# Last two stages of a conditioned residual stack fused over batch rows, with the residual kept time-innermost

## The chip, the cores and the metric

The kernel runs on one core of one Trainium2 chip. The metric is the device time of one execution, in microseconds (us); before the change it is the median of 3 runs. The profile is one further execution, taken by the hardware profiler. Engines are named as in the profile: PE (TensorE's matmuls), PEld (TensorE's weight loads), DVE (VectorE), ACT (ScalarE), POOL (GpSimd), SP (SyncE, which issues most DMAs).

## The reference

The input x is (16, 512, 512): batch B, time T, channels D, all float32; `cond` is (16, 512). Four layers are applied, each added to x:

```
x = x + ssm(x)      # causal conv (4 taps), softplus/tanh gates of 64 states, linear scan over time, projection to D
x = x + lstm(x)     # a = x Wx + h Wh + b; i,f,o = sigmoid, g = tanh; c = f c + i g; h = o tanh(c); h0 = cond
x = x + moe(x)      # below
x = x + masked(x)   # below

def moe(x):         # E=16 experts, slot = e_idx*C + position, C = 512, rows past capacity are dropped
    xprev = concat([cond[:, None], x[:, :-1]], axis=1)
    xk, xr = x + (xprev - x) * maa_k, x + (xprev - x) * maa_r
    rows = zeros(E*C + 1, D).at[slot].set(xk)
    out  = square(relu(rows @ w_key)) @ w_value          # per expert
    return sigmoid(xr @ w_recept.T) * out[slot]

def masked(x):      # over time, for each batch row and channel
    ax = abs(x);  pi = exp(2 * ax / sum(ax));  cum = cumsum(pi / sum(pi)) + 0.001
    chosen = sum(cum <= rv)                              # rv = cond
    return x * (ax >= ax[chosen])
```

The residual after the LSTM is called x2 below, after the experts x3. The last layer needs, for each batch row and channel, all 512 times of x3.

## The kernel before, in words

Four stages run one after the other, with a barrier over all engines at the end of each. Channels lie on the 128 partitions in KD = 4 blocks. Within an engine instructions run in the order in which they are written in its list; engines hand over by semaphores. Loops over tiles are hardware loops (`Fori`) with the first and last tiles unrolled. Large fp32 products of tiles are made from three fp32r products of a high and a low part (`split_products`, L837 to L842).

**`recur_phase`** (L105 to L834) walks through time in 32 tiles of 16 steps; a tile has 256 tokens, time-major (t, b). Each LSTM step, in two halves of the hidden channels, is a chain: PE's recurrent products (`recur`, L425), VectorE's transposes out of PSUM (`turn`, L696) and sum with the input products (`add_inputs`, L701), ScalarE's tanh (L586, L587), VectorE's cell (`new_cell`, L707 to L713), ScalarE's tanh of it (L589), VectorE's hidden state (`new_hidden`, L718), and back to PE. All else is put beside it as filler, by tables that say in which step of a tile each piece is issued: `CONV_AT` (convolution products L625/L629 for the tile three ahead, on VectorE), `SCAN_AT` (five parts of the state scan, L635 to L667), `BLOCK_AT` (`add_block` L683, first residual sum into the `stream` tile), `SPLIT_AT` (high part L523 on ACT; POOL makes the low part, `split_low` L293), `KEEP_X2_AT` (`keep_x2` L691: x2 into the stream tile, one instruction of 512 elements for each half tile), `PROJECT_AT`, `INPUTS_AT`, `OUTPUTS_AT` (PE's products, L375 to L396), ACT's copy of the input products (`keep_inputs` L528, every step), and, for the tile before, `SCALE_AT`, `TURN_AT`, `ROWS_AT`: the token shift for the experts. That shift is, for each half tile: POOL subtracts (`mix_shift` L303), ACT scales (`scale_shift` L534), POOL adds (`mix_add` L308), PE transposes to token rows (`turn_rows` L406), ACT copies them out (`keep_rows` L542), POOL scatters them to the expert rows in DRAM by the slot table (`scatter`, L315 and L321). There are four `stream` tiles in a ring, (KD, 16 + 256): the 16 leading columns, the halo, are the last time of the tile before, copied by POOL (L341). SP stores each tile's x2 to DRAM in its token order (L238) and loads the windows of later tiles.

**`expert_phase`** (L845 to L1035) multiplies the 16 experts. It is not changed.

**`combine_phase`** (L1038 to L1251, "gating stage") walks over 32 tiles of 256 tokens: ACT and VectorE mix the token with the one before, split it in high and low parts, PE makes the receptance in three products of four blocks, each in its own PSUM bank, ACT the sigmoid (L1194), POOL gathers expert rows by the slot table, PE transposes them, VectorE multiplies and adds into x3, which stays in SBUF, (KD, B, T) with time innermost (`times`; written at a stride, L1246).

**`mask_phase`** (L1254 to L1425, "last stage") walks over 64 units, one batch row and channel block each, of 512 times: ACT takes |x| and its sum (L1335), VectorE halves and inverts the sum (L1378, L1384), ACT makes the exponent into PSUM with its sum (L1343), VectorE the running sum (`scan` L1388) and the threshold (`bound` L1394), ACT counts times below the threshold by the sum of signs (L1351), VectorE turns that into an index (L1408), picks the value at it (`search` L1413) and makes the factor 1 or 2 (L1420), POOL multiplies (L1326), SP stores (L1306).

## Time and profile before

| | us |
|---|---|
| median of 3 runs (range) | 4221.14 (4220.53 to 4221.26) |
| the profiled execution | 4221.9 |
| its span | 4220.2 |
| PE busy in the span | 3814.3 (90%) |
| DVE busy | 3103.0 (74%) |
| ACT busy | 1798.7 (43%) |
| POOL busy | 590.7 (14%) |

The span runs from the first to the last recorded instruction. The shares are means over stages with different limits, so rows are given by stretch below. The recurrence runs from 122 to 3013 us, the experts up to 3808, the gating stage from there to 4036.6, the last stage to the end. Busy PE is not PE at its peak; "granted clock" (PEclk) is the share of its full clock that TensorE was given.

### The profile page before, as it was taken

To read this page: it belongs to the slowest core of one execution; us is meant where nothing else is said; L and a number is where in the kernel's file an instruction comes from. 1 tells how busy PE (TensorE), PEld (TensorE's weight loads), DVE (VectorE), ACT (ScalarE), POOL (GpSimd) and SP (SyncE) were. 2 spreads that over 40 slices of the span, in tenths; PEclk is the share of its full clock that TensorE was granted. 3 is DMA by queue.
4 is the path that set the end of the run, shared out by engine and by line. 5 is a ranking of instruction groups with operands and counts; after the bars stand their busy time and mean duration, and the time that the engine had idled before them with its cause. 6 is when DMAs were issued, how large, how long until landed. Compare 5 with 4: busy or idle time off the path is not lost. (4 is left out here: it accounts for less than half of the span.)

```text
span 4220.2 us, 116142 instructions
## 1 busy us (share of the span) xinstructions
PE 3814.3 (90%) x45058; PEld 2616.4 (62%) x45058; DVE 3103.0 (74%) x9922; ACT 1798.7 (43%) x5526; POOL 590.7 (14%) x653
## 2 busy tenths in 40 slices
PE   3999999999999999999999999999599999997920
PEld 3566666666656666665666666665378887887920
DVE  9877888787878787887878788855455445537989
ACT  3334333334333334433333433333244344437877
POOL 2011101111101110110111110110100000004644
PEclk9999999999999999999999999999899999998965
DMA  7110010110010110010001001000233433324422
GB/s 276 31 36 27 29 31 27 34 36 27 29 32 27 32 39 27 26 34 27 29 31 36 27 29 31 25 21 12 94 131 122 161 135 119 122 84 156 164 83 97
DMA packets 143096, 267.78 MB, mean 63 GB/s; under 512 B 19606, under 2 KB 85654, under 8 KB 139540
## 3 DMA queue, kind: packets, MB, share of 16 engines
q1 hardware_dynamic: 120896, 185.19, 13.1%
q0 software_dynamic: 17696, 66.79, 4.3%
q10 hardware_dynamic: 4020, 9.10, 0.6%
q8 instruction: 335, 5.49, 0.6%
q14 instruction: 149, 1.22, 0.1%
HBM read 177.46 MB, written 83.92 MB: 62 GB/s over the span
## 5 line engine op out<-in xcount | busy, mean ns | idle before, releaser
L425 PE MATMUL bank<-buf,buf 128*16 128x256 f32 x32768 | 1871.9, 380 | 78.5 <-DVE buf L718 65.4
L425 PEld LDWEIGHTS bank<-buf,buf 128*16 128x16 f32 x32768 | 905.9, 97 | 903.3 <-DVE buf L718 116.0
L840 PE MATMUL bank<-buf,buf 128*128 128x256 f32 (+1 forms) x3584 | 1183.1, 330 | 29.8 <-DVE buf L1225 22.4
L841 PE MATMUL bank<-buf,buf 128*128 128x256 f32 (+1 forms) x3584 | 1122.7, 313 | 0.0
L842 PE MATMUL bank<-buf,buf 128*128 128x256 f32 (+1 forms) x3584 | 1122.3, 313 | 0.0
L629 DVE SCALAR_TENSOR_TENSOR buf<-buf,buf,buf 128x256 f32<-128x256 f32 x1920 | 871.9, 481 | 1.6 <-issue 1.6
L840 PEld LDWEIGHTS bank<-buf,buf 128*128 128x128 f32 x3584 | 678.9, 189 | 279.9 <-issue 241.8
L696 DVE STREAM_TRANSPOSE buf<-bank 128x256 f32<-128x256 f32 x1024 | 459.0, 448 | 510.3 <-PE bank L425 479.7
L586 ACT ACTIVATE buf<-buf 128x96 f32<-128x96 f32 x1024 | 290.5, 284 | 1161.5 <-DVE buf L701 1160.9
L842 PEld LDWEIGHTS bank<-buf,buf 128*128 128x128 f32 x3584 | 680.5, 190 | 41.2
L841 PEld LDWEIGHTS bank<-buf,buf 128*128 128x128 f32 x3584 | 681.7, 190 | 38.5
L589 ACT ACTIVATE buf<-buf 128x32 f32<-128x32 f32 x1024 | 235.0, 229 | 628.2 <-DVE buf L713 628.2
L701 DVE SCALAR_TENSOR_TENSOR buf<-buf,buf 128x128 f32<-128x128 f32 x1024 | 368.6, 360 | 20.0
L1023 DVE CAST buf<-buf 128x512 fp32r<-128x512 f32 x128 | 54.7, 427 | 355.6 <-ACT buf L983 352.5
L308 POOL TENSOR_TENSOR buf<-buf,buf 128x512 f32<-128x512 f32 x64 | 81.8, 1279 | 1477.1 <-ACT buf L534 1477.1
L528 ACT ACTIVATE buf<-bank,buf 128x256 f32<-128x256 f32 x512 | 234.7, 458 | 21.9 <-PE bank L842 20.9
L718 DVE SCALAR_TENSOR_TENSOR buf<-buf,buf 128x32 f32<-128x32 f32 x1024 | 194.2, 190 | 61.4 <-ACT buf L589 14.2
L713 DVE SCALAR_TENSOR_TENSOR buf<-buf,buf 128x32 f32<-128x32 f32 x1024 | 196.6, 192 | 36.6 <-DVE buf L710 1.4
L587 ACT ACTIVATE buf<-buf 128x32 f32<-128x32 f32 x1024 | 217.9, 213 | 0.0
L707 DVE SCALAR_TENSOR_TENSOR buf<-buf,buf 128x32 f32<-128x32 f32 x1024 | 179.5, 175 | 18.2 <-ACT buf L586 15.1
L710 DVE SCALAR_TENSOR_TENSOR buf<-buf,buf 128x32 f32<-128x32 f32 x1024 | 190.0, 186 | 0.0
L293 POOL TENSOR_TENSOR buf<-buf,buf 128x512 fp32r<-128x512 f32 x64 | 82.1, 1284 | 559.3 <-ACT buf L523 559.3
(143 smaller groups left out, 3040.3 us busy)
## 6 DMA issues: line engine op xcount, KB each, us to landing
buf<-in_wk SPq DMA_DIRECT2D x16, 2048.0 KB, 9.6
buf<-in_wv SPq DMA_DIRECT2D x16, 2048.0 KB, 9.7
buf<-in_xT SPq DMA_DIRECT2D x62, 496.0 KB, 3.8
buf<-x_scratch SPq DMA_DIRECT2D x31, 544.0 KB, 4.2
buf<-in_xT SPq DMA_DIRECT2D x32, 512.0 KB, 3.7
expert_in_scratch<-buf POOLq DMA_DIRECT2D x16, 1024.0 KB, 22.2
x_scratch<-buf SPq DMA_DIRECT2D x32, 512.0 KB, 5.0
buf<-expert_in_scratch SPq DMA_DIRECT2D x16, 1024.0 KB, 11.6
```

Of the source, the lines that this page charges most:

```text
L425: last = mm(gate_ps[hf][32 * j:32 * j + B, 0:HCOLS], hist[:, k, at_step(slot_at)], wh[:, k, j * GCOLS + hf * HCOLS:j * GCOLS + (hf + 1) * ...
L528: a(xw[par][:, :, q, :], xw_ps[q % 2][:, 0:LTILE].rearrange("p (t b) -> p t b", b=B), ACT.Identity, bias=bias[:, q:q + 1]).then_inc(s["xw_ ...
L586: a(gate[hf], pre[hf][:, 0:6, :], ACT.Tanh, scale=0.5).then_inc(s["ifo_ready"][hf], 1)
L587: a(gcand[hf], pre[hf][:, 6:8, :], ACT.Tanh).then_inc(s["g_ready"][hf], 1)
L589: a(tanh_c[hf], cell[hf], ACT.Tanh, scale=0.5).then_inc(s["tc_ready"][hf], 1)
L629: v.scalar_tensor_tensor(out=conv[:, k, :], in0=src, scalar=taps[:, k, i:i + 1], in1=conv[:, k, :], op0=ALU.mult, op1=ALU.add).then_inc(s[ ...
L696: v.transpose(turned_g[hf].rearrange("p g b -> p (g b)"), gate_ps[hf][:, 0:HCOLS])\
L701: v.scalar_tensor_tensor(out=pre[hf], in0=turned_g[hf][:, :, 0:B], scalar=0.5, in1=xw[par][:, st, 8 * hf:8 * hf + 8, :], op0=ALU.mult, op1 ...
L713: v.scalar_tensor_tensor(out=cell[hf], in0=term_f[hf], scalar=0.5, in1=term_i[hf], op0=ALU.mult, op1=ALU.add).then_inc(s["c_ready"][hf], 1)
L840: nc.tensor.matmul(out, left[0], right[0], start=first, stop=False)
L841: nc.tensor.matmul(out, left[0], right[1], start=False, stop=False)
L842: return nc.tensor.matmul(out, left[1], right[0], start=False, stop=last)
```

## The change

`x2` in DRAM becomes (partition, channel block, batch row, time), and the `stream` tiles (KD, B, 1 + 16): time innermost, rows of 17 words with the halo as the first. All that writes or reads them follows: tokens of a tile are now ordered (b, t) for the input, state and mixing products, while the recurrence's own history and convolution stay time-major, so some operands are read at a stride. SP's store of a tile's x2 becomes 8192 runs of 64 bytes. The token shift is made by ACT (`weigh_last`: last times maa_k) and VectorE (`mix_in`: now times 1 - maa_k, plus that), four instructions each for a half tile; the low parts of the split go from POOL to VectorE; `keep_x2` is four instructions a half. POOL keeps the halo copies and scatters. The slot table is reloaded in (b, t) order, and a second one, `place`, in batch-row order.

`combine_phase` and `mask_phase` go; `finish_phase` takes their place, fully unrolled over the 16 batch rows, with a ring of six row buffers. Its receptance is plain fp32 products of 512 columns (in four passes of PE) into two banks, without splits; the sigmoid is a tanh of half the value, with the halving in VectorE's product. ACT's Tanh and Exp, VectorE's scans and POOL's products of neighbouring rows are interleaved in written-out orders.

```diff
-    x2_d = nc.dram_tensor("x2_scratch", (KD, P, NTOK), F32, kind="Internal").ap()
+    x2_d = nc.dram_tensor("x2_scratch", (P, KD, B, T), F32, kind="Internal").ap()
...
-    stream = [carve(KD, B + LTILE) for _ in range(4)]
+    stream = [carve(KD, B, 1 + LSTEPS) for _ in range(4)]
...
-    CONV_AT = [[0, 5, 10, 15, 18, 21, 24, 28, 32], [0, 4, 9, 14, 18, 21, 24, 29, 32]]
+    CONV_AT = [[0, 5, 10, 15, 18, 21, 24, 28, 32], [0, 5, 10, 13, 17, 20, 23, 27, 32]]
...
-    SCALE_AT, TURN_AT, ROWS_AT = (4, 10), (5, 13), (6, 14)
+    SCALE_AT, MIX_AT, TURN_AT, ROWS_AT = (4, 9), (5, 10), (6, 13), (7, 14)
+    LOW_AT = (13, 14)
...
+            sp.dma_start(place, slot_d.rearrange("(c p) -> p c", p=P), allow_slow_non_contiguous=True)\
...
-                    sp.dma_start(x2_d.rearrange("c p n -> p c n")[:, :, bass.ds((n - 1) * LTILE, LTILE)],
-                                 stream[four - 1][:, :, B:]).then_inc(s["x2_stored"][(four + 1) % 2], 16)
+                    sp.dma_start(x2_d.rearrange("p c b t -> p (c b) t")[:, :, bass.ds((n - 1) * LSTEPS, LSTEPS)],
+                                 stream[four - 1].rearrange("p c b t -> p (c b) t")[:, :, 1:])\
...
-                g.tensor_tensor(mix, stream[four][:, :, u * P:u * P + P], stream[four][:, :, B + u * P:B + u * P + P],
-                                ALU.subtract).then_inc(s["shift_ready"], 1)
...
             def keep_inputs(m, par, q):
-                a(xw[par][:, :, q, :], xw_ps[q % 2][:, 0:LTILE].rearrange("p (t b) -> p t b", b=B), ACT.Identity,
+                a(xw[par][:, :, q, :], xw_ps[q % 2][:, 0:LTILE].rearrange("p (b t) -> p t b", b=B), ACT.Identity,
...
+            def weigh_last(m, four, u):
+                for k in range(KD):
+                    a(mix[:, k, :].rearrange("p (b t) -> p b t", b=B), stream[four][:, k, :, 8 * u:8 * u + 8],
+                      ACT.Copy, scale=maa_k[:, k:k + 1])\
...
             def keep_x2(n, four, u):
-                v.scalar_tensor_tensor(out=kept, in0=hist[:, :, tok], scalar=0.5, in1=kept, op0=ALU.mult,
-                                       op1=ALU.add).then_inc(s["x2_done"], 1)
+                for k in range(KD):
+                    kept = stream[four][:, k, :, 8 * u + 1:8 * u + 9]
+                    last = v.scalar_tensor_tensor(
+                        out=kept, in0=hist[:, k, u * P:(u + 1) * P].rearrange("p (t b) -> p b t", b=B), scalar=0.5,
+                        in1=kept, op0=ALU.mult, op1=ALU.add)
...
+            def mix_in(m, four, u):
+                for k in range(KD):
+                    part = mix[:, k, :].rearrange("p (b t) -> p b t", b=B)
+                    v.scalar_tensor_tensor(out=part, in0=stream[four][:, k, :, 8 * u + 1:8 * u + 9],
+                                           scalar=maa_now[:, k:k + 1], in1=part, op0=ALU.mult,
+                                           op1=ALU.add).then_inc(s["mixed"], 1)
...
+def finish_phase(nc, ctx, ins, carve, banks, keep, x2_d, y_d, out):
+    RING, NC = 6, T // P
+    r_ps, t_ps, pi = banks[0:2], banks[2:6], banks[6:8]
...
+            def receptance(i):                                             # PE
+                pe.wait_ge(s["xr_ready"], KD * (i + 1))
+                for m in range(KD):
+                    if i >= 1 or m >= 2:
+                        pe.wait_ge(s["gate_ready"], KD * i + m - 1)
+                    for k in range(KD):
+                        last = nc.tensor.matmul(r_ps[m % 2][:, 0:T], wr[:, k, m * P:(m + 1) * P], xr[i % 2][:, k, :],
+                                                start=k == 0, stop=k == KD - 1)
+                    last.then_inc(s["r_summed"], 1)
...
+            receptance(0)
+            turn(0)
+            receptance(1)
+            turn(1)
+            receptance(2)
+            for i in range(B):
+                if i + 2 < B:
+                    turn(i + 2)
+                if i + 3 < B:
+                    receptance(i + 3)
...
+            def open_gate(i):                                              # ACT
+                for m in range(KD):
+                    act.wait_ge(s["r_summed"], KD * i + m + 1)
+                    a(gate[i % 2][:, m, :], r_ps[m % 2][:, 0:T], ACT.Tanh, scale=0.5).then_inc(s["gate_ready"], 1)
...
+            def exponent(i):                                               # ACT
+                act.wait_ge(s["inv_ready"], i + 1)
+                for k in range(KD):
+                    if i >= 1 or k >= 2:
+                        act.wait_ge(s["cum_ready"], KD * i + k - 1)
+                    a(pi[k % 2][:, 0:T], ax[i % 2][:, k, 0:T], ACT.Exp, scale=column(inv, i, k),
+                      accum_out=column(pi_sum, i, k)).then_inc(s["pi_ready"], 1)
...
+            for i in range(B):                                             # ACT
+                take_sides(i)
+                if i + 1 < B:
+                    absolute(i + 1)
+                if i + 2 < B:
+                    open_gate(i + 2)
+                if i + 1 < B:
+                    exponent(i + 1)
+                if i + 4 < B:
+                    weigh_last(i + 4)
...
+            def combine(i):                                                # DVE
+                for k in range(KD):
+                    u = KD * i + k
+                    dve.wait_ge(s["gate_ready"], u + 1)
+                    dve.wait_ge(s["turned"], u + 1)
+                    v.scalar_tensor_tensor(out=gated[k % 2], in0=gate[i % 2][:, k, :], scalar=1.0, in1=t_ps[k][:, 0:T],
+                                           op0=ALU.add, op1=ALU.mult).then_inc(s["gated_ready"], 1)
+                    dve.wait_ge(s["gated_ready"], u + 1)
+                    v.scalar_tensor_tensor(out=x2_of(i, k), in0=gated[k % 2], scalar=0.5, in1=x2_of(i, k),
+                                           op0=ALU.mult, op1=ALU.add).then_inc(s["x3_ready"], 1)
...
+            for i in range(B):                                             # DVE
+                scan(i)
+                bound(i)
+                if i + 1 < B:
+                    combine(i + 1)
+                if i + 3 < B:
+                    mix_in(i + 3)
+                choose(i)
+                if i + 1 < B:
+                    invert(i + 1)
+                search(i)
+                keep(i)
```

`scan`, `bound`, `choose`, `search` and `keep` do for the four blocks of a row what the old stage did for a unit. POOL gathers the expert rows of row i + 3, then makes the four products of row i; SP loads a row's x2 as soon as its ring buffer is free and stores each finished block.

## Rows read from the trace of the kernel before

**Rows 1.** Windows by stage: stretch, us, busy us of PE, PEld, DVE, ACT, POOL, PEclk, DMA share, GB/s.
```profile
122.00:3013.00 2891.00, 2815.33 (x39600) 1760.76 (x39600) 2239.94 (x8305) 1108.62 (x4210) 316.28 (x340) 1.00 0.09 29
3808.30:4036.60 228.30, 210.80 (x1792) 210.38 (x1792) 202.71 (x293) 185.78 (x357) 126.30 (x129) 0.96 0.48 156
4036.60:4220.20 183.60, 0.00 (x0) 0.00 (x0) 170.97 (x513) 143.99 (x385) 82.35 (x70) 0.50 0.24 91
```
**Rows 2.** Timeline in one recurrence tile: start, us, instruction, count, [idle before, releaser].
```profile
1336.47 0.65 DVE L640 SCALAR_TENSOR_TENSOR buf<-bank,buf,buf 64x256 f32<-64x256 f32 x1
...
1337.85 0.45 DVE L696 STREAM_TRANSPOSE buf<-bank 128x256 f32<-128x256 f32 x1 [0.72 <-PE bank L425]
...
1343.04 0.45 DVE L696 STREAM_TRANSPOSE buf<-bank 128x256 f32<-128x256 f32 x1
1343.53 1.84 DVE L701 SCALAR_TENSOR_TENSOR buf<-buf,buf 128x128 f32<-128x128 f32 x1
1343.90 1.30 POOL L303 TENSOR_TENSOR buf<-buf 128x512 f32<-128x512 f32 x1
...
1349.94 0.44 DVE L696 STREAM_TRANSPOSE buf<-bank 128x256 f32<-128x256 f32 x1
...
1383.28 0.45 DVE L696 STREAM_TRANSPOSE buf<-bank 128x256 f32<-128x256 f32 x1 [1.71 <-PE bank L425]
...
1389.68 0.45 DVE L696 STREAM_TRANSPOSE buf<-bank 128x256 f32<-128x256 f32 x1 [1.67 <-PE bank L425]
...
1393.09 0.48 DVE L629 SCALAR_TENSOR_TENSOR buf<-buf,buf,buf 128x256 f32<-128x256 f32 x1
1393.48 0.68 DVE L691 SCALAR_TENSOR_TENSOR buf<-buf,buf 128x512 f32<-128x512 f32 x1
...
1394.73 0.45 DVE L696 STREAM_TRANSPOSE buf<-bank 128x256 f32<-128x256 f32 x1 [0.57 <-PE bank L425]
1395.29 0.79 DVE L701 SCALAR_TENSOR_TENSOR buf<-buf,buf 128x128 f32<-128x128 f32 x1
```
**Rows 3.** VectorE's groups, 150 to 2740 us: count | busy us, mean ns | idle before.
```profile
L629 DVE SCALAR_TENSOR_TENSOR buf<-buf,buf,buf 128x256 f32<-128x256 f32 x1711 | 785.9, 481 | 1.6 <-issue 1.6
L691 DVE SCALAR_TENSOR_TENSOR buf<-buf,buf 128x512 f32<-128x512 f32 x57 | 38.7, 679 | 0.0
L640 DVE SCALAR_TENSOR_TENSOR buf<-bank,buf,buf 64x256 f32<-64x256 f32 x29 | 18.8, 648 | 0.0
L635 DVE TENSOR_TENSOR buf<-buf,buf 64x256 f32<-64x256 f32 x29 | 11.9, 410 | 0.0
```
**Rows 4.** Timeline: the gating stage's first work, the last scan.
```profile
3814.32 2.19 ACT L1162 ACTIVATE buf<-buf 128x512 fp32r<-128x512 f32 x4 [14.29 <-DMA buf<-in_maa_r]
...
4211.31 1.21 DVE L1388 TENSOR_TENSOR_SCAN buf<-buf,bank 128x512 f32<-128x512 f32 x1
```
**Rows 5.** Groups by line and shape over the whole span, last stage.
```profile
L1413 DVE SCALAR_TENSOR_TENSOR buf<-buf,buf,buf 128x513 f32<-128x513 f32 x64 | 48.8, 762 | 0.0
L1343 ACT ACTIVATE bank<-buf,buf 128x512 f32<-128x512 f32 x64 | 44.2, 691 | 27.2 <-DVE buf L1384 27.2
L1420 DVE TENSOR_SCALAR buf<-buf,buf 128x512 f32<-128x512 f32 x64 | 31.1, 487 | 0.9
```
**Rows 6.** PE's timeline in one recurrence tile.
```profile
1312.25 1.03 PE L375 MATMUL bank<-buf,buf 128*128 128x256 f32 x4
```
**Rows 7.** Windows around two pauses of PE, columns as in rows 1.
```profile
58.10:61.90 3.80, 0.01 (x1) 0.01 (x1) 3.80 (x5) 1.23 (x2) 2.69 (x3) 0.80 0.36 116
61.90:67.20 5.30, 5.28 (x25) 5.30 (x26) 5.30 (x15) 0.47 (x1) 5.30 (x10) 0.50 0.84 325
...
3821.80:3825.20 3.40, 3.37 (x16) 3.40 (x17) 1.67 (x4) 2.79 (x6) 0.00 (x0) 0.50 0.40 94
```
**Rows 8.** The page's DMA issues: count, KB each, median us from issue to landing.
```profile
buf<-in_wk SPq DMA_DIRECT2D x16, 2048.0 KB, 9.6
```
**Rows 9.** The page's DMA queues: packets, MB, share of 16 engines' span.
```profile
q1 hardware_dynamic: 120896, 185.19, 13.1%
```

More of the change, by code:

```diff
@@ L522, in split_high @@
                     act.wait_ge(s["xw_summed"], NBLK * (m - 1))
[L523 removed]
+                a(x1_hi[four % 2][:, two(q), :].rearrange("p k (b t) -> p (k b) t", b=B),
+                  stream[four][:, two(q), :, 1:].rearrange("p k b t -> p (k b) t"), ACT.Copy)\
                     .then_inc(s["x1_hi_ready"], 1)
@@ L796, in _ @@
             for q in range(2):
+                split_low(0, 0, q)
+            for q in range(2):
                 convolve(1, q, 0, CONVS // 2)
@@ L802, in _ @@
                 add_block(1, 0, 1, q)
+            for q in range(2):
+                split_low(1, 1, q)
             convolve(2, 1, 0, CONVS // 2)
@@ L830, in tile @@
                         add_block(n + 2, pair + 1, (four + 2) % 4, BLOCK_AT.index(st))
+                    if ahead >= 2 and st in LOW_AT:
+                        split_low(n + 2, (four + 2) % 4, LOW_AT.index(st))
+                    if later(n, 1) and st in MIX_AT:
+                        mix_in(n - 1, (four - 1) % 4, MIX_AT.index(st))
                     if st in KEEP_X2_AT:
@@ L834, in _ @@
             tiles(dve, tile)
+            for u in range(2):
+                mix_in(NLT - 1, 3, u)
 def split_products(nc, out, left, right, first, last):
@@ L1156, in _, with turn @@
-            tiles(pe, tile)
+            def turn(i):
+                for c in range(NC):
+                    pe.wait_ge(gathered[NC * (i % 2) + c], 16 * (i // 2 + 1))
+                for k in range(KD):
+                    if i >= 1:
+                        pe.wait_ge(s["gated_ready"], KD * (i - 1) + k + 1)
+                    for c in range(NC):
+                        last = nc.tensor.transpose(t_ps[k][:, c * P:(c + 1) * P],
+                                                   rows[i % 2][c][:, k * P:(k + 1) * P], ident)
+                    last.then_inc(s["turned"], 1)
@@ L1199, in _, with weigh_last @@
-            tiles(act, tile)
+            a = nc.scalar.activation
+            def weigh_last(i):
+                act.wait_ge(landed[i % RING], 16 * (i // RING + 1))
+                act.wait_ge(s["halo_ready"], i + 1)
+                for k in range(KD):
+                    if i >= 1:
+                        act.wait_ge(s["xr_ready"], KD * (i - 1) + k + 1)
+                    a(weighed[:, k, :], stream[i % RING][:, k, 0:T], ACT.Copy, scale=maa_r[:, k:k + 1])\
+                        .then_inc(s["weighed"], 1)
@@ new lines, in _ @@
+            act.wait_ge(s["weights_landed"], 32)
+            weigh_last(0)
+            weigh_last(1)
+            open_gate(0)
+            weigh_last(2)
+            absolute(0)
+            open_gate(1)
+            exponent(0)
+            weigh_last(3)
+            for i in range(B):
+                take_sides(i)
[7 more added lines that the diff above has]
+                    weigh_last(i + 4)
@@ new lines, in bound, with choose, search @@
+            def bound(i):
+                dve.wait_ge(s["cum_ready"], KD * (i + 1))
+                v.tensor_tensor(limit[i % 2], rv[:, :, i], pi_sum[i % 2], ALU.mult).then_inc(s["limit_ready"], 1)
+            def choose(i):
+                dve.wait_ge(s["sides_ready"], KD * (i + 1))
+                v.tensor_scalar(chosen[i % 2], sides[i % 2], 0.5, T / 2, ALU.mult, ALU.add)\
+                    .then_inc(s["chosen_ready"], 1)
+            def search(i):
+                dve.wait_ge(s["chosen_ready"], i + 1)
+                for k in range(KD):
+                    v.scalar_tensor_tensor(out=flag[:, k, :], in0=places, scalar=column(chosen, i, k), in1=ax[i % 2][:, k, :],
+                                           op0=ALU.is_equal, op1=ALU.mult, accum_out=column(level, i, k))\
+                        .then_inc(s["level_ready"], 1)
```

539 lines of the change are left out of this document (176 added, 363 removed).

## The prediction

> **What bounds the kernel now.** I read the busy times by stage first, then the vector engine's timeline inside one tile of the recurrence, then the last two stages. The page's 90% for PE hides three limits. The recurrence takes 2891 of 4220.2 us; PE runs at full clock, but each of its 512 steps is a chain PE, VectorE, ScalarE, VectorE, PE, and VectorE has about 22% idle [rows 1]. The gating stage takes 228.3 us, 210.8 of them PE; the last stage takes 183.6 us without PE, VectorE busy for 171.0 [rows 1]. So a bound by PE is followed by one by VectorE, and overlapping them is what can be won. The expert stage between is untouched.
>
> **The recurrence, part by part.** A plain step lasts 5.19 us, from one first transpose L696 to the next (1337.85 to 1343.04) [rows 2]; I number steps 0 to 15 in a tile. Step 7 lasts 6.90 (from 1343.04), since L701 takes 1.84 (at VectorE's rate, below, it is worth 0.28) while POOL's subtraction L303 runs for 1.30, and the fill behind it then ends late [rows 2]. Step 14 carries the same kind of extra PE products without that block and lasts 6.40 (1383.28 to 1389.68); step 15 lasts 5.05 [rows 2].
> Removed: six POOL products of this kind a tile. Step 7 falls to step 14's 6.40, so -0.5; the blocked L701 of step 0 (0.79 instead of 0.28) gives back some 0.4 [rows 2].
> Moved: PE's row transposes from step 5 to 6, which I take as neutral. Step 5 would then last 5.19, but VectorE gets four mixing products (128 elements, pointer scalar). L629 takes 0.481 for 256; L691 and L635 differ by 0.269 for 256 elements, 1.05 ns each, so 128 elements take 0.347 [rows 3]. Neighbours overlap by some 0.08 (L629 of 1393.09 takes 0.48, and L691 behind it starts after 0.39 [rows 2]), so four take 1.14. They stand behind L640 (1336.47, minus the 0.45 by which step 5's own block shifts it), so step 5 ends 0.3 later than 5.19.
> Step 15: two more convolution products, 0.4 each, move L691's place from 1393.48 to 1394.28 [rows 2], and its second half becomes four instructions of 128. L691 takes 0.679 for 512 [rows 3], so 0.28 for 128, 0.20 apart. One operand is now read at a stride of 64 bytes; L640, which writes at that stride, takes 0.648 for 256 where L635 takes 0.410, of which 0.06 is the pointer scalar [rows 3]: some 0.6 ns an element, so 0.08 each. The four start 0.28 apart and the last takes 0.36, so they end at 1395.48; the next transpose, at 1394.73 before, overlaps them by 0.08 and starts 0.67 late.
> Steps 10 to 14 also get work (four products, the residual sums at up to 1.0, two splits of 0.68), within the 0.5 to 1.7 us that VectorE waits for PE there: at 1389.68 it had waited 1.67 [rows 2]. Without that cover they would cost 3 us a tile.
>
> Sum a tile: -0.5 - 0.4 + 0.3 + 0.67 = +0.07, times 28 tiles +2 us. Bounds: stride for nothing gives -8; every stream operand (rows of 17 words) at the stride's price +20. I take +2. ScalarE's copies of input products read PSUM at a 64-byte stride; only those ahead of the table loads in step 3 lie on the path: 0 to 0.15 x 28; I take all of it, +4. The start has four more VectorE splits and fewer POOL blocks: -3 to +4, taken as 0. At the end the last scatter no longer waits for two pairs of POOL products, 1.3 each, replaced by VectorE's 1.1, partly overlapped: -3. SP also issues each tile's residual store, now 8192 runs of 64 bytes, and a second slot table; window loads queued behind have some 40 us to spare, and the last store lies beside the scatters (priced among the rivals). Recurrence: +3 us.
>
> **The fused stage.** One batch row (512 tokens) replaces two gating tiles and four mask units. VectorE per row: four mixing products 0.66 apart (2.7), four dependent pairs at 0.60 each and 0.11 for the operand in PSUM, an estimate (5.3, from L691 [rows 3]), four scans 1.13 apart (4.6, L1388 [rows 4]), four searches 0.70 apart (2.8, L1413 [rows 5]), four factors (1.6, L1420 [rows 5]), small ones 0.8: 17.8 us. PE: an fp32 product is four passes; two of 256 columns are the four records of L375 in 1.03, 0.43 each to issue [rows 6], so 0.86 for 512; sixteen make 13.8, transposes about 2: 15.8 at full clock. ScalarE: twenty instructions at 0.6 to 0.7 (L1343 [rows 5]): 13.
>
> None of these sets the period; the order does. ScalarE's order is sides of row i, absolute of i+1, gate of i+2, exponent of i+1. Receptance has two banks, so PE stops after two blocks of row i+2 until ScalarE has opened gate 0, and gates 2 and 3 then wait for PE, one after the other, with the exponent queued behind them and VectorE's scan behind that. The cycle: scan 4.6, limit 0.25, combine 5.3, last absolute 0.7, gate 0 0.6, two PE blocks 6.9, gate 3 0.6, first exponent 0.75, six hand-overs 0.4 (estimate) = 20.1 us. VectorE's mixing, search and factors (7.5) run beside PE's blocks. The added wait is this one, and PE itself idles 20.1 - 15.8 = 4.3 us a row.
>
> That idle time costs clock. After 3.80 us without a product PE is at 0.50 for the next 5.3 us; at the gating stage's first products it is at 0.50 for 3.4 us [rows 7]. Half speed over 3.4 us puts 1.7 us on the two blocks, which lie on the cycle: 21.8 us a row (22.7 with the 5.3).
>
> Start: the weights were there at 3814.3 [rows 4]; one more MB loads ahead of them, half of the 9.6 us that 2 MB take [rows 8]: 3819.1. Mixing 3.4, receptance of row 0 13.8 + 1.7 at half clock, transposes 2, receptance of row 1 13.8, gate 0.8, exponent 0.75: first scan at 3855.4. Row 15's scan follows 14 periods and one short iteration (no gate left: 15.9) later. From the last scan to the end the old kernel needs 4220.2 - 4211.3 = 8.9 [rows 4]; with four units in each step 3 x (1.13 + 0.72 + 0.70 + 1.27) more: 20.4. End: 3855.4 + 14 x 21.8 + 15.9 + 20.4 = 4196.9, so 411.9 has become 388.6.
>
> **Sum.** 4196.9 + 3 = 4199.9. The profiled execution took 4221.9, 1.7 beyond its span and 0.8 above the median of 4221.14, so I forecast 4202 us, 0.45% less.
>
> **Rivals.**
> First, the clock holds, as gaps below 4.3 us may go unpunished: 20.1 a row, 4197 - 24 + 5 = 4178. Against it stands the drop after 3.80 us [rows 7]. Bound 4165.
> Second, the small stores cost like other packets. The page's main queue spends 13.1% of 16 engines' span on 120896 packets, 73 ns each [rows 9]; 8192 / 16 such packets take 37 us. Within a tile of 90 us that hides, but the last store then lands near 3055 and the stage, which ended at 3035 (new: 3032), waits: +23, so 4225. No row shows writes of 64 bytes. The Trainium skill (DMA: Bandwidth & Descriptors, Specifications) speaks against this layout too: below 512 bytes a transfer does a read-modify-write, so each 64-byte run would cost a read beside its write. By that rule the last store is at least late in this way, and no row of this trace shows it.
> Third, slower: PE's clock does not come back within the two blocks. Place: blocks 2 and 3 of each row's receptance. If PE stays at half for both, they take 13.8 instead of 6.9, the period is 27.0, and the time 3891.7 + 14 x 27.0 + 4.7 = 4274. It decides from 23.3 us a row, where PE is at half for 6.3 us after each gap; the rows have 3.4 and 5.3 [rows 7], which speaks against it, but never with a gap in every row.
> Fourth, the strided operands cost their upper bound: +18, 4220, no change.
>
> POOL's final products (1.3 each) may hold up VectorE's factors as L303 holds up L701 [rows 2]: at most 3.8 on 17.8, still below 21.8, so it would show only beside rival 1, as 21.6 a row.
>
> **Chances.** Forecast 47% (its own range 4190 to 4215, the upper end at 22.7 a row), rival 1 18%, rival 2 10%, rival 3 13%, rival 4 7%, something else 5%. No change means within 0.2%, 8.4 us, about what a measurement of this kernel can tell: 4212.7 to 4229.6. Faster: 44 + 18 + 1 = 63%; same: 3 + 9 + 6 = 18%; slower: 13 + 1 + 1 + 4 = 19%. For 8 in 10 the range goes from inside rival 1 to past rivals 2 and 4: 4168 to 4234.
>
> **What would show it.** After: scans of successive rows 21 to 22 us apart; PE idle some 4 us in each, ended by ScalarE's gate, and the granted clock below 1.0 there; ScalarE waiting for PE in two of four gates; VectorE idle before each row's first scan; L701 never above 0.4 except beside POOL's short copies; step 15 near 5.7, step 7 near 6.4; the expert stage beginning within 5 us of 3035. Rows 20 us apart at full clock mean rival 1; a gap of 20 us before the expert stage, ended by the residual's store, rival 2; rows 24 us or more apart rival 3. I am wrong in kind if VectorE has no idle time in the fused stage, or if the recurrence moves by more than 20 us.

## The result, and the profile after

The changed kernel takes 4194.43 us (median of 4 runs, 4192.25 to 4197.63) where the kernel before takes 4221.2 (4220.53 to 4221.46): a ratio of 0.9937, 95% interval 0.992 to 0.9955, 27 us less. The forecast was 4202 with a range of its own of 4190 to 4215, so the time lies inside. The stages show that two terms missed it in opposite directions, by 17 and by 11 us. The table compares the two traced executions; the one traced after the change is the slowest of its four, 3.2 us above their median, so its spans differ by 25.3 us and not by 27.

| us, from the two traces | before | after | forecast of the difference |
|---|---|---|---|
| first step's first transpose | 121.98 | 120.34 | 0 |
| last step's first transpose | 3008.68 | 2997.42 | +6 |
| expert stage's first load | 3035.49 | 3021.67 | +3, measured -13.8 |
| first DMA behind the experts | 3808.37 | 3795.01 | +3 |
| from there to the end | 411.8 | 399.9 | -23.3, measured -11.9 |
| span | 4220.2 | 4194.9 | -20, measured -25.3 |

The expert stage between is as long as before (772.9 and 773.3). First two windows of the kernel after: the recurrence, and the rows of the fused stage from the first row's first scan to the last row's (stretch, us, busy us of PE, PEld, DVE, ACT, POOL, PEclk, DMA share, GB/s). They answer to [rows 1].

```profile
120.34:3002.60 2882.26, 2815.95 (x39600) 1761.56 (x39600) 2316.79 (x8808) 1111.99 (x4212) 83.91 (x156) 1.00 0.14 29
3844.90:4156.00 311.10, 252.14 (x675) 119.79 (x674) 261.14 (x445) 178.67 (x445) 123.73 (x118) 0.88 0.37 125
```

In the recurrence VectorE has 77 us more to do and POOL 232 us less, in a slightly shorter stretch. In the 311 us of rows no engine is full: VectorE, which is busy for 84%, comes nearest, and PE's granted clock is 0.88.

VectorE's timeline in the same tile as [rows 2], transposes that begin steps 5, 6, 7, 8, 14, 15 and the next step 0, and the residual sums in step 15:

```profile
1327.21 0.45 DVE L682 STREAM_TRANSPOSE buf<-bank 128x256 f32<-128x256 f32 x1 [0.84 <-PE bank L387]
1332.60 0.43 DVE L682 STREAM_TRANSPOSE buf<-bank 128x256 f32<-128x256 f32 x1
1338.04 0.45 DVE L682 STREAM_TRANSPOSE buf<-bank 128x256 f32<-128x256 f32 x1 [0.30 <-PE bank L387]
1344.47 0.45 DVE L682 STREAM_TRANSPOSE buf<-bank 128x256 f32<-128x256 f32 x1 [0.41 <-PE bank L387]
...
1377.82 0.45 DVE L682 STREAM_TRANSPOSE buf<-bank 128x256 f32<-128x256 f32 x1 [1.10 <-PE bank L387]
1384.23 0.45 DVE L682 STREAM_TRANSPOSE buf<-bank 128x256 f32<-128x256 f32 x1 [1.46 <-PE bank L387]
...
1388.82 1.20 DVE L659 SCALAR_TENSOR_TENSOR buf<-buf,buf 128x128 f32<-128x128 f32 x4
1389.94 0.44 DVE L682 STREAM_TRANSPOSE buf<-bank 128x256 f32<-128x256 f32 x1
```

Steps 5, 6, 7, 14 and 15 last 5.39, 5.44, 6.43, 6.41 and 5.71. By medians over the tiles (before, then after): step 0 5.53 and 5.15, step 5 5.64 and 5.38, step 6 5.19 and 5.45, step 7 6.91 and 6.44, step 15 5.06 and 5.72; all others within 0.03. A tile goes from 90.30 to 90.12.

VectorE's groups in the recurrence, 150 to 2740 us (count | busy us, mean ns | idle before): the sum of the chain that was held up (L701 before, L687 now), the residual sums and the mixing products.

```profile
L701 DVE SCALAR_TENSOR_TENSOR buf<-buf,buf 128x128 f32<-128x128 f32 x912 | 330.7, 363 | 17.7
...
L687 DVE SCALAR_TENSOR_TENSOR buf<-buf,buf 128x128 f32<-128x128 f32 x916 | 264.7, 289 | 18.9 <-DVE buf L682 1.4
L659 DVE SCALAR_TENSOR_TENSOR buf<-buf,buf 128x128 f32<-128x128 f32 x228 | 68.2, 357 | 0.0
L676 DVE SCALAR_TENSOR_TENSOR buf<-buf,buf,buf 128x128 f32<-128x128 f32 x224 | 62.8, 339 | 0.0
```

Before the change 82 of the 912 sums took over 0.15 us longer than their median of 0.29, 67 us in all; after it none does. The held sums stand in step 0 (0.40 longer), step 7 (1.55) and, which the prediction's sum leaves out, step 5: there POOL's second product of the shift held a sum in each of 28 tiles, by 0.45. From the same tile before:

```profile
1332.01 1.28 POOL L308 TENSOR_TENSOR buf<-buf,buf 128x512 f32<-128x512 f32 x1 [26.46 <-ACT buf L534]
...
1332.69 0.75 DVE L701 SCALAR_TENSOR_TENSOR buf<-buf,buf 128x128 f32<-128x128 f32 x1
```

Now the fused stage. VectorE's first scans of three rows, and PE's and ScalarE's timeline between them:

```profile
3978.51 4.55 DVE L1274 TENSOR_TENSOR_SCAN buf<-buf,bank 128x512 f32<-128x512 f32 x4 [3.70 <-ACT bank L1203]
...
4000.12 4.55 DVE L1274 TENSOR_TENSOR_SCAN buf<-buf,bank 128x512 f32<-128x512 f32 x4 [2.57 <-ACT bank L1203]
...
4022.87 1.22 DVE L1274 TENSOR_TENSOR_SCAN buf<-buf,bank 128x512 f32<-128x512 f32 x1 [3.72 <-ACT bank L1203]
```
```profile
3976.98 1.91 PE L1154 MATMUL bank<-buf,buf 128*128 128x128 f32 x16
3978.72 7.03 PE L1143 MATMUL bank<-buf,buf 128*128 128x512 f32 x16
3989.94 8.81 PE L1143 MATMUL bank<-buf,buf 128*128 128x512 f32 x16 [4.19 <-ACT buf L1188]
3998.59 1.91 PE L1154 MATMUL bank<-buf,buf 128*128 128x128 f32 x16
4000.34 7.03 PE L1143 MATMUL bank<-buf,buf 128*128 128x512 f32 x16
4011.56 9.94 PE L1143 MATMUL bank<-buf,buf 128*128 128x512 f32 x16 [4.19 <-ACT buf L1188]
```
```profile
3989.32 1.05 ACT L1188 ACTIVATE buf<-bank 128x512 f32<-128x512 f32 x2
3995.36 0.60 ACT L1188 ACTIVATE buf<-bank 128x512 f32<-128x512 f32 x1 [4.99 <-PE bank L1143]
3998.79 0.60 ACT L1188 ACTIVATE buf<-bank 128x512 f32<-128x512 f32 x1 [2.84 <-PE bank L1143]
3999.28 0.69 ACT L1203 ACTIVATE bank<-buf,buf 128x512 f32<-128x512 f32 x1
```

This is the cycle of the prediction, step for step: PE makes two blocks, stops for 4.19 us until ScalarE opens gate 0 (the tanh of the receptance's first block); two more blocks follow, gates 2 and 3 wait for them (4.99 and 2.84), the exponent stands behind gate 3 and VectorE's scan, idle for 2.6 or 3.7, behind the exponent. Rows come 21.61 and 22.75 us apart, in turn. The same two blocks take 7.03 in one place and 8.81 or 9.94 behind the pause. The windows of two pauses and of what follows them:

```profile
3985.80:3989.90 4.10, 0.00 (x0) 0.00 (x0) 4.03 (x8) 4.10 (x14) 0.00 (x0) 1.00 0.13 46
3989.90:3993.40 3.50, 3.46 (x4) 1.51 (x5) 3.46 (x11) 0.47 (x1) 0.00 (x0) 0.51 0.00 0
...
4007.40:4011.50 4.10, 0.00 (x0) 0.00 (x0) 4.03 (x8) 4.10 (x14) 0.00 (x0) 0.87 0.12 50
4011.50:4018.20 6.70, 6.64 (x9) 2.90 (x10) 6.67 (x18) 0.58 (x3) 1.83 (x2) 0.57 0.00 0
```

The granted clock is at the lower level (1.2 of 2.4 GHz) for 3.5 us behind one pause and for most of 6.7 behind the next. Where it held at the upper level (an experiment below) gate 3 came 7.80 us behind gate 0; here 9.46 or 10.60, so the clock costs 1.66 or 2.80 a row.

### The profile page after: what moved, and what is told of

Same layout as the page of the kernel before. It is cut to its first block and busy times, and to the rows that moved or that the text cites. A ratio compares the mean times of both kernels' runs of the same rounds, so it can differ in the third digit from the quotient of the medians.

```text
span 4194.9 us, 112126 instructions
## 1 busy us (share of the span) xinstructions
PE 3890.3 (93%) x44034; PEld 2542.4 (61%) x44034; DVE 3109.5 (74%) x10143; ACT 1679.4 (40%) x5296; POOL 289.2 (7%) x410
## 3 DMA queue, kind: packets, MB, share of 16 engines
q1 hardware_dynamic: 366416, 184.21, 16.4%
## 5 line engine op out<-in xcount | busy, mean ns | idle before, releaser
L837 PE MATMUL bank<-buf,buf 128*128 128x256 f32 (+1 forms) x3072 | 1037.1, 338 | 4.0 <-DVE buf L1008 2.7
L838 PE MATMUL bank<-buf,buf 128*128 128x256 f32 (+1 forms) x3072 | 979.0, 319 | 0.0
L839 PE MATMUL bank<-buf,buf 128*128 128x256 f32 (+1 forms) x3072 | 978.4, 318 | 0.0
L837 PEld LDWEIGHTS bank<-buf,buf 128*128 128x128 f32 x3072 | 582.0, 189 | 254.6 <-issue 216.3
L839 PEld LDWEIGHTS bank<-buf,buf 128*128 128x128 f32 x3072 | 583.9, 190 | 41.2
L838 PEld LDWEIGHTS bank<-buf,buf 128*128 128x128 f32 x3072 | 584.7, 190 | 38.5
L1143 PE MATMUL bank<-buf,buf 128*128 128x512 f32 x512 | 259.6, 666 | 85.2 <-ACT buf L1188 59.0
L687 DVE SCALAR_TENSOR_TENSOR buf<-buf,buf 128x128 f32<-128x128 f32 x1024 | 295.9, 289 | 21.0 <-DVE buf L682 1.4
L1143 PEld LDWEIGHTS bank<-buf,buf 128*128 128x128 f32 x512 | 107.5, 216 | 226.0 <-issue 155.5
L704 DVE SCALAR_TENSOR_TENSOR buf<-buf,buf 128x32 f32<-128x32 f32 x1024 | 193.7, 189 | 61.7 <-ACT buf L557 14.2
L298 POOL DMA_INDIRECT expert_in_scratch<-buf,buf x64 | 63.4, 991 | 2415.3 <-ACT buf L510 2372.5
L699 DVE SCALAR_TENSOR_TENSOR buf<-buf,buf 128x32 f32<-128x32 f32 x1024 | 196.7, 192 | 35.9 <-DVE buf L696 0.6
L693 DVE SCALAR_TENSOR_TENSOR buf<-buf,buf 128x32 f32<-128x32 f32 x1024 | 177.5, 173 | 17.9 <-ACT buf L554 14.8
## 6 DMA issues: line engine op xcount, KB each, us to landing
expert_in_scratch<-buf POOLq DMA_DIRECT2D x16, 1024.0 KB, 22.7
```

What stands on the lines that cost most here:

```text
L687: v.scalar_tensor_tensor(out=pre[hf], in0=turned_g[hf][:, :, 0:B], scalar=0.5, in1=xw[par][:, st, 8 * hf:8 * hf + 8, :], op0=ALU.mult, op1 ...
L837: nc.tensor.matmul(out, left[0], right[0], start=first, stop=False)
L838: nc.tensor.matmul(out, left[0], right[1], start=False, stop=False)
L839: return nc.tensor.matmul(out, left[1], right[0], start=False, stop=last)
L1143: last = nc.tensor.matmul(r_ps[m % 2][:, 0:T], wr[:, k, m * P:(m + 1) * P], xr[i % 2][:, k, :], start=k == 0, stop=k == KD - 1)
```

## The experiments

Each ratio is to the kernel before on the same chip, whose own median lay between 4220.2 and 4223.8 from group to group of runs; the changed kernel's own ratio is 0.9937. Times of different groups are compared with the changed kernel's 4194.4, so differences of 2 or 3 us between groups are not read.

### Which part gave what

The changed recurrence with the old last stages:

```diff
-        finish_phase(nc, ctx, ins, carve, banks, keep, x2_d, y_d, out)
+        combine_phase(nc, ctx, ins, carve, banks, keep, x2_d, y_d)
+        mask_phase(nc, ctx, carve, banks, keep, out)
...
-    x2v = x2_d.rearrange("c p n -> p c n")
+    x2v = x2_d.rearrange("p c b t -> p c (b t)")
```

> The changed recurrence with the gating stage and the last stage of before behind it; the gating stage reads the residual's new layout as if it were the old one, so the values are not the reference's, the work is. Theory (the two parts add, read from the stage bounds of the two traces: expert stage starts at 3021.7 instead of 3035.5, last two stages 399.9 instead of 411.9): the expert stage starts within 1.5 us of 3021.7, the last two stages take 412 again, the time is 4221.2 - 13.8 = 4207 us (4204 to 4211). Rival (the recurrence as the prediction had it, +3): 4224. Rival (all of the gain is in the fused stage, the earlier expert start is of this one profile): 4221.

4208.03 us, ratio 0.9965 (0.9952 to 0.9977), 15 us less than before. The expert stage starts at 3018.1, 3.6 us ahead of the expected 3021.7 where 1.5 was allowed, and the last two stages take 412.8 again. So somewhat over half of the gain is the recurrence's, for which the prediction had +3.

### What holds the rows of the fused stage

First the clock. PE's transposes are moved into the pause, so that the pause becomes short:

```diff
                 for m in range(KD):
+                    if m == 2:
+                        turn(i)
                     if i >= 1 or m >= 2:
```

> The changed kernel with PE's transposes of a row moved from behind its receptance to between its blocks 1 and 2, into the pause of 4.19 us. Theory (the pause costs clock: blocks 2 and 3 take 1.9 or 3.0 us more than at full clock): the pause shrinks to about 1.5 us, the granted clock stays at 1.00, blocks 2 and 3 take 6.9 to 7.0 us, rows come 19.7 us apart instead of 21.6 and 22.75, and the time is 4194.4 - 14 x 2.45 = 4160 us (4156 to 4166). Rival (the transposes stand on the cycle themselves, no clock): rows 20.4 apart with blocks as long as before, 4170. Rival (neither counts, PE has 2.6 us of room elsewhere): 22.2 us a row, 4194.

4196.12 us, 0.9937 (0.992 to 0.9953): no change. The theory in this form fell. PE's timeline and windows around gate 0:

```profile
3981.56 0.63 PE L1156 MATMUL bank<-buf,buf 128*128 128x128 f32 x4
3982.79 0.66 PE L1156 MATMUL bank<-buf,buf 128*128 128x128 f32 x4 [0.61 <-DVE buf L1249]
3984.12 0.66 PE L1156 MATMUL bank<-buf,buf 128*128 128x128 f32 x4 [0.67 <-DVE buf L1249]
3985.44 0.66 PE L1156 MATMUL bank<-buf,buf 128*128 128x128 f32 x4 [0.67 <-DVE buf L1249]
3987.45 15.70 PE L1145 MATMUL bank<-buf,buf 128*128 128x512 f32 x32 [1.36 <-ACT buf L1182]
```
```profile
3981.50:3987.45 5.95, 2.62 (x17) 1.68 (x16) 5.85 (x10) 5.95 (x19) 0.00 (x0) 1.00 0.13 44
3987.45:3994.40 6.95, 6.95 (x12) 2.96 (x13) 6.92 (x17) 1.02 (x2) 2.12 (x2) 0.75 0.00 0
4003.10:4009.09 5.99, 2.65 (x17) 1.68 (x16) 5.89 (x10) 5.99 (x19) 0.01 (x1) 0.93 0.36 128
4009.09:4016.00 6.91, 6.91 (x10) 2.91 (x11) 6.88 (x17) 0.66 (x2) 2.09 (x2) 0.57 0.00 0
```

No pause is longer than 1.36 us, and yet the clock falls to 0.75 and 0.57 over the next 6.9 us: ahead of gate 0 PE worked for 2.6 of 5.9 us. Two of its rows came 19.93 us apart, the others 21.6 to 23.0. That left it open whether the clock is the cause at all. So the pause was filled instead, with products whose results nobody reads:

```diff
                     if m == 2:
+                        if i >= 1:
+                            pe.wait_ge(s["gated_ready"], KD * (i - 1) + 1)
+                            nc.tensor.matmul(t_ps[0][:, 0:T], wr[:, 0, 0:P], xr[i % 2][:, 0, 0:T], start=True, stop=True)
...
                         turn(i)
```

> The kernel with the transposes in the pause, and ahead of them PE products whose results nobody reads (two of 512 columns and one of 256, into a transpose bank that is free by then), so that PE has no pause left before gate 0. Theory (what the rows lose is clock; with the transposes alone the clock still fell in most rows, because PE was busy in only 2.6 of the 5.9 us ahead of gate 0, and the one row group where it held came 19.9 us apart): the granted clock stays at 1.00 from row to row, blocks 2 and 3 take 6.9 us, rows come 19.7 us apart, time 4194.4 - 14 x 2.5 = 4160 us (4156 to 4166), though PE does 2.1 us more work a row. Rival (the length of blocks 2 and 3 has another cause, such as the order of waits around gate 0): 21.6 to 23.0 a row as before, 4195. Rival (more work on PE delays gate 2): above 4195.

4166.86 us, 0.9874 (0.9858 to 0.9891), 28 us below the changed kernel, though PE does more. The window over the whole of its rows, and one pause that is filled:

```profile
3812.30:4126.30 314.00, 288.32 (x855) 139.60 (x853) 271.92 (x462) 189.94 (x469) 127.72 (x122) 1.00 0.39 136
```
```profile
3990.60:3996.70 6.10, 4.49 (x24) 2.88 (x23) 5.96 (x11) 6.10 (x19) 1.47 (x2) 1.00 0.66 246
3996.70:4003.60 6.90, 6.90 (x16) 3.12 (x17) 6.87 (x17) 0.99 (x2) 2.11 (x2) 1.00 0.00 0
```

The clock stays at 1.00 throughout, and rows come 19.94 us apart, 13 of 14 within 0.07. Against the run before it only PE products and a wait ahead of them were added, so the clock is shown to be what the rows lost. That is the cycle at full clock. The expected 19.7 had taken the cost of the clock from PE's merged durations (1.9 and 3.0); from gate 0 to gate 3 it is 1.66 and 2.80, and 21.61 and 22.75 less these are 19.95.

Then ScalarE's order, which makes the cycle:

```diff
-                if i + 2 < B:
-                    open_gate(i + 2)
-                if i + 1 < B:
-                    exponent(i + 1)
+                for blocks in ((0, 1), (2, 3)):
+                    if i + 2 < B:
+                        open_gate(i + 2, blocks)
+                    if i + 1 < B:
+                        exponent(i + 1, blocks)
```

> The changed kernel with ScalarE's order gates 0 and 1, exponents 0 and 1, gates 2 and 3, exponents 2 and 3, instead of four gates and four exponents. Theory (the cycle runs through gates 2 and 3 that stand ahead of the exponents): the first scan of a row no longer waits for them; VectorE, 19.0 us busy a row with its waits for POOL's products, becomes the limit, or exponent 2 behind gate 3 at 19.7 to 20.8 where the clock still falls. Rows 19.0 to 20.3 us apart, time 4194.4 - 14 x (2.0 to 3.2) = 4150 to 4167 us, middle 4158. Rival (PE's slow clock sets the rows, whatever ScalarE's order): 22.2 us a row, 4194.

4156.17 us, 0.9843 (0.9826 to 0.9859): 38 us below the changed kernel, by two exponents a row put ahead of two gates. Rows come 19.1 apart on the mean. The window shows the new bound: VectorE is busy for 195.4 of 200 us, with the clock still at 0.94: rows are 18.95 apart where it holds and up to 19.4 where it falls.

```profile
3900.00:4100.00 200.00, 175.20 (x504) 84.50 (x503) 195.44 (x331) 134.02 (x332) 94.94 (x90) 0.94 0.43 152
```

Both of these edits together:

> The changed kernel with both orders (transposes in the pause, exponents 0 and 1 ahead of gates 2 and 3), POOL's products where the change has them. Theory (VectorE sets the rows, 19.0 us with the factors waiting for POOL's products): rows 19.0 us apart, factors 0.90 us on the mean, time 4194.4 - 14 x 3.15 = 4150 us (4146 to 4156). Rival (the products cost nothing in any order, as in the changed kernel, where VectorE has 2.6 to 3.7 us idle a row): 17.5 a row, 4130.

4158.84 us, 0.9848 (0.982 to 0.9877): no better than the early exponents alone. Rows at 18.95 are there, but between them some of 20.8 to 21.0, where the clock fell, so the mean is 19.2. The expected 19.0 had left the clock out.

With VectorE as the bound, POOL's products count, which hold up the factors (0.897 us on the mean in the changed kernel's rows, 0.487 before [rows 5]):

```profile
L1298 DVE TENSOR_SCALAR buf<-buf,buf 128x512 f32<-128x512 f32 x56 | 46.8, 897 | 0.0
```

```diff
-                    pool.wait_ge(s["factor_ready"], KD * i + k + 1)
+                    pool.wait_ge(s["factor_ready"], KD * i + (KD if i + 1 < B else k + 1))
```

> Both of these orders together, and POOL's four products of a row held back until VectorE has made all four factors, so that they run beside its scans (in the trace of before 62 scans ran beside such products at 1.205 us, as long as without). Theory (then VectorE alone sets the rows; a factor takes 0.49 instead of 0.90 us without the products beside it): rows 17.4 to 17.8 us apart, VectorE without idle time, time 4194.4 - 14 x 4.6 = 4130 us (4124 to 4138). Rival (the products block VectorE wherever they stand, then its products of gate and rows): 19.0 a row, 4150. Rival (PE or the clock still sets the rows): 19.7 or more, above 4158.

> The kernel with exponents 0 and 1 ahead of gates 2 and 3 and late products, the transposes where the change has them. Theory (moving the transposes gained nothing in the changed kernel and lost 2.7 us beside the early exponents; late products take 1.6 us a row from VectorE): 4156.2 - 14 x (1.0 to 1.6) = 4134 to 4143 us. Rival (the clock falls in every row and sets the rows by gate 3 and exponent 2): 19.0 a row, 4154.

4142.73 (0.9809, 0.9793 to 0.9826) with both orders, 4141.11 (0.9813, 0.9797 to 0.9829) with the transposes left in place. The late products are worth 16 us behind both orders and 13 to 15 behind the early exponents alone, the move of the transposes again nothing. Rows are 17.66 apart where the clock holds and 19.4 where it falls; with both orders the time is above the expected 4124 to 4138, which had taken the clock to hold. At last all of these edits together, with two unread PE products of 512 columns a row in the pause:

> The kernel with both orders and late products, and two PE products of 512 columns that nobody reads ahead of the transposes in the pause. Theory (its rows were 17.66 apart where the clock held and 19.4 where it fell, mean 18.2): all rows 17.7 apart, VectorE busy in 17.3 of them, time 4142.7 - 14 x 0.55 = 4135 us (4131 to 4140). Rival (PE, now busy for 17.3 us a row, becomes late itself): 18.2 or more, 4143 or above.

4136.32 us, 0.98 (0.9784 to 0.9816), the fastest of all, 58 us below the changed kernel. Windows, and VectorE's factors and scans and POOL's products in the same stretch:

```profile
3900.00:4100.00 200.00, 195.14 (x580) 95.25 (x578) 191.47 (x357) 142.01 (x354) 96.39 (x96) 1.00 0.44 157
```
```profile
L1273 DVE TENSOR_TENSOR_SCAN buf<-buf,bank 128x512 f32<-128x512 f32 x47 | 54.8, 1206 | 5.2 <-ACT bank L1201 5.2
L1297 DVE TENSOR_SCALAR buf<-buf,buf 128x512 f32<-128x512 f32 x48 | 20.0, 480 | 0.0
...
L1129 POOL TENSOR_TENSOR buf<-buf,buf 128x512 f32<-128x512 f32 x48 | 55.2, 1182 | 92.5 <-DVE buf L1297 92.5
```

The factors are back at 0.48, and the scans, beside which the products now run, take 1.206, no longer than the 1.20 of the changed kernel. PE and VectorE are both at 96 to 98%, and VectorE is idle for under 0.8 us a row, so another order has little left to win.

### What moved in the recurrence

The row transposes of the first half, in steps 8 and 9 instead of 6 and 7 (`TURN_AT`, `ROWS_AT`):

```diff
-    SCALE_AT, MIX_AT, TURN_AT, ROWS_AT = (4, 9), (5, 10), (6, 13), (7, 14)
+    SCALE_AT, MIX_AT, TURN_AT, ROWS_AT = (4, 9), (5, 10), (8, 13), (9, 14)
```

> The changed kernel with the first half's row transposes in step 8 and their copy in step 9, instead of 6 and 7. Theory (the transposes cost the step that holds them 0.25 us of the chain, which the prediction took as nothing): step 6 falls from 5.45 to 5.20, step 8 rises from 5.07 to some 5.3, step 7 stays at 6.44, the time unchanged within 3 us. Rival (step 6 is longer for another reason, VectorE's mixing products in step 5): step 6 stays at 5.45. Rival (step 7's extra length is ScalarE's row copy): step 7 falls below 6.3.

4194.5 us, 0.9928 (0.9906 to 0.9951), no change in time. Step 6 falls from 5.45 to 5.06, step 7 from 6.44 to 6.19, step 8 rises from 5.07 to 5.65. The transposes do cost the step that holds them; that step 7 falls as well may be due to the copy, as the last rival has it, or to what step 6 had left over, which this run does not tell apart.

The strided operand, taken away in one place (the history is read contiguously):

```diff
-                        out=kept, in0=hist[:, k, u * P:(u + 1) * P].rearrange("p (t b) -> p b t", b=B), scalar=0.5,
+                        out=kept, in0=hist[:, k, u * P:(u + 1) * P].rearrange("p (b t) -> p b t", b=B), scalar=0.5,
```

> The changed kernel with the history operand of the residual sums read contiguously instead of at a stride of 64 bytes (other tokens' values, so the output is not the reference's; same count of instructions and elements). Theory (the stride costs VectorE some 0.08 us for 128 elements, and step 15 waits for it): the sums take 0.28 instead of 0.357 us, step 15 lasts 5.72 - 0.32 = 5.40, 28 tiles make -9 us: 4185. Rival (their length is from the pointer or the short rows of the other operand): 0.357 and 5.72 stay, 4194.

4185.6 us, 0.9912 (0.9883 to 0.994). The residual sums take 0.282 instead of 0.357, step 15 5.41 instead of 5.72, a tile 0.33 less: theory and number hold. The group in the recurrence:

```profile
L659 DVE SCALAR_TENSOR_TENSOR buf<-buf,buf 128x128 f32<-128x128 f32 x232 | 51.5, 282 | 0.0
```

POOL's work was put back in two pieces. The low-part subtraction (`split_low`), again on POOL:

```diff
-                    if ahead >= 2 and st in LOW_AT:
-                        split_low(n + 2, (four + 2) % 4, LOW_AT.index(st))
...
+                g.tensor_tensor(x1_lo[four % 2][:, two(q), :].rearrange("p k (b t) -> p (k b) t", b=B),
...
+                if ahead >= 2:
+                    for q in range(2):
+                        split_low(n + 2, (four + 2) % 4, q)
```

> The changed kernel with the two low-part subtractions of a tile back on POOL, in the place in its order where they were before; the token shift stays on ScalarE and VectorE. Theory (POOL's products held up VectorE's sums; VectorE's own splits in steps 13 and 14 are hidden behind its wait for PE): steps 13 and 14 stay at 5.65 and 6.41, some of the 32 pairs of POOL products hold up a sum of the chain by 0.5 to 1.5 us, about +0.3 us a tile, the recurrence 5 to 15 us longer, 4204. Rival (POOL's products cost the chain nothing where PE is late anyway): 4194, unchanged.

4194.64 us, 0.993 (0.9907 to 0.9952), unchanged. Its 58 products are there, and not one sum of the chain is held up:

```profile
L291 POOL TENSOR_TENSOR buf<-buf,buf 128x512 fp32r<-128x512 f32 x58 | 69.4, 1197 | 962.7 <-ACT buf L502 962.7
...
L697 DVE SCALAR_TENSOR_TENSOR buf<-buf,buf 128x128 f32<-128x128 f32 x915 | 264.5, 289 | 17.9
```

The theory fell for this pair: it neither cost nor gained. The trace shows why: all 58 lie in steps 12 and 13, and none of them beside a sum of the chain. In the kernel before its 56 (L293) lay in the same two steps, beside no sum either, so the sums that were held up there were held by the shift's products alone. The token shift (`mix_shift`, `mix_add`), again on POOL, without VectorE's mixing products:

```diff
+            def mix_shift(m, four, u):
+                g.tensor_tensor(mix_all(), shifted(four, 8 * u), shifted(four, 8 * u + 1),
+                                ALU.subtract).then_inc(s["shift_ready"], 1)
...
-                        mix_in(n - 1, (four - 1) % 4, MIX_AT.index(st))
```

> The changed kernel with the token shift of the experts back on POOL (one subtraction and one sum for a half tile, ScalarE scaling in between) instead of ScalarE and VectorE; the low-part split stays on VectorE. Theory (POOL's products of the shift, not those of the split, held up VectorE's sums of the chain): the sums are held up again, 0.36 us on the mean instead of 0.289, step 7 goes from 6.44 to 6.9, step 0 from 5.15 to 5.5, step 5 loses its four mixing products and falls to 5.2; a tile takes 90.12 + 0.46 + 0.38 - 0.18 = 90.8 us, the time 4194.4 + 28 x 0.66 + 3 for the end = 4216 us (4205 to 4220). Rival (the holding up came from the layout of before or from chance in the phase of POOL's work): no sum held up, step 5 shorter, 4190.

4253.8 us, 1.0078 (1.0062 to 1.0095): slower than before by 0.8%, and 59 us above the changed kernel where 22 were expected. A tile takes 92.12 us, step 0 6.02, step 7 7.23. Two places of its timeline:

```profile
578.96 1.06 POOL L299 TENSOR_TENSOR buf<-buf 128x512 f32<-128x512 f32 x1
578.98 1.20 DVE L698 SCALAR_TENSOR_TENSOR buf<-buf,buf 128x128 f32<-128x128 f32 x1
...
1550.74 1.95 DVE L679 SCALAR_TENSOR_TENSOR buf<-buf,buf 128x128 f32<-128x128 f32 x2
...
1551.43 1.09 POOL L299 TENSOR_TENSOR buf<-buf 128x512 f32<-128x512 f32 x1
```

From 150 to 2740 us 55 sums of the chain are over 0.15 us longer than their median (in step 0 by 0.90, in step 5 by 0.50), and 24 residual sums (L679, step 7, by 1.30) besides, 69 us in all; in the kernel before it was 82 sums and 67 us. The kind of theory holds; the expectation had not counted the residual sums, nor step 5, which lasts 5.55 and not 5.2 although its mixing products are gone. So in this layout the recurrence gains 2.0 us a tile by having the shift off POOL.

## Why the prediction was right, and where it was not

**What bounds the kernel, and that overlapping is what can be won:** right. In the rows VectorE is busy for 84% and PE for 81% at once, where the old last stage left PE idle throughout.

**The recurrence, +3 forecast, -13.8 measured: wrong in sign.** The step that failed is the sum for step 5. The prediction saw the block there (the 0.45 by which "step 5's own block" shifts L640) and wrote that step 5 would then last 5.19, but its sum counts only the blocks of steps 7 and 0 as removed and adds 0.3 on top of 5.19. Step 5 had lasted 5.64, so the sum should have had 5.49 - 5.64 = -0.15 in place of +0.3; measured it is -0.26. The release left out is 0.45 x 28 = 12.6 us, and the mixing products cost 0.19 instead of 0.3, another 3. Against that stand PE's transposes, moved "as neutral": they cost step 6 0.26, 7 us. Together steps 5 and 6 last as long as before (10.83 us) where +0.3 was forecast, 8 us over the tiles. The other terms: step 7's -0.5 came as -0.47, step 0's -0.4 as -0.38, step 15's +0.67 as +0.66, with the stride's price from L640 confirmed by the experiment (0.075 for 128 elements; 0.08 was forecast). ScalarE's strided PSUM copies, +4, cost nothing: 457 ns a copy, 458 before. Not counted at all: the start is 1.6 us shorter and the last three tiles 3.6; no run shows the cause of these two. The tail had -3 and got -2.6 (from the last step to the expert loads 26.8, now 24.25). The 8, 4, 1.6 and 3.6, less 0.4 of the tail, are the 16.8 us of the miss.

**The fused stage, -23.3 forecast, -11.9 measured: right in mechanism, four sizes short.** The period at full clock was forecast as 20.1 and is 19.94. The clock's price was 1.7 a row and is 1.66 in one row and 2.80 in the next, so 22.2 instead of 21.8: 14 rows, 6 us. The prediction had both lengths, 21.8 and 22.7, as alternatives; the rows have them in turn, and no run shows why. The first scan came 49.9 us behind the first DMA instead of 47.0, as the weights landed 13.5 us behind it and not 10.7; the last row took 17.1 instead of 15.9; the end 21.8 instead of 20.4.

**The forecast of 4202 therefore stands on two errors that cancel,** 16.8 us too much and 11.4 too little. That the time came so close is luck; the time alone hides both. A smaller slip stands in its last step: by its own figures 4199.9 + 1.7 - 0.8 is 4200.8, not 4202. Of the signs that it named, the expert stage beginning within 5 us of 3035 failed (3021.7).

**The rivals.** The clock held in no row of the changed kernel; filling the pause shows what it would be worth, 28 us, close to the 24 of that rival. The slow clock in both blocks did not come either, but the rows with the longer stretch, every second one, are near its point (23.3 us a row; these have 22.75). The small stores cost nothing that can be seen: a tile's store lands 9.2 us after its issue instead of 5.0, and the expert stage begins 24 us behind the last step, sooner than before. The queue's row, beside [rows 9]:

```profile
q1 hardware_dynamic: 366416, 184.21, 16.4%
```

245,520 packets more took 16.4% x 16 x 4194.9 - 13.1% x 16 x 4220.2 = 2160 us of engine time, 8.8 ns each, where that rival had 73. The Trainium skill (DMA: Bandwidth & Descriptors, Specifications) had spoken against this layout, since below 512 bytes a read-modify-write takes place; no run here separates such a price from the 8.8 ns that these 64-byte writes cost in all. The strides cost their middle value, not the upper bound.

**POOL's products before VectorE's factors** were said to show only beside the first rival. In the changed kernel a row has 4 x 0.41 = 1.6 us of it, which VectorE's idle time covers; they cost 13 to 16 us as soon as VectorE is the bound. The Trainium skill (SBUF — State Buffer, Who interferes with whom) says that VectorE and GpSimd take turns at a shared pair of ports, whoever comes first keeps it for the whole instruction, and that a VectorE instruction with at most one SBUF operand outside the two-port modes is exempt. The traces agree for sums with two SBUF operands (L698, 1.20 instead of 0.29), which were held, and for scans with one operand out of PSUM (1.206), which were not. The factors (1.04 beside a product, 0.48 without) were held too; that they run in a two-port mode no run shows.

## What to carry to other kernels

When a cause is taken away, look in the trace for every place where it stood, and take what each step lasted there as the base of the sum: the block left out in step 5 was worth 12.6 us, about as much as the whole gain of the recurrence (13.8). Where an in-order engine serves two chains, put first what the bound engine waits for and only then what waits for another engine; and where PE has a wait in every round that a clock drop follows, products that nobody reads can be cheaper than the pause (28 us here). Check a total that came out right by stage, since two errors may have met in it.

## What the runs showed of the hardware that was not expected

The granted clock fell not only behind pauses of 4.19 us but also behind 5.9 us with four groups of transposes and no pause over 1.36 us, and it did not fall behind 6.1 us in which PE was busy for 4.49. Behind pauses of one length it stayed low for 3.5 us and for most of 6.7 in turn, which goes with rows of two lengths. ScalarE reads PSUM at a stride of 64 bytes at no cost that shows (457 ns against 458), while VectorE pays 0.075 us for 128 elements read from SBUF at that stride.
